# Edge columns of 128 instead of 125 in a graph network kernel

## The chip, the core and the metric
The kernel runs on one core of a Trainium2 chip. TensorE (PE) multiplies matrices, VectorE (DVE) and ScalarE (ACT) compute element by element, GpSimd (POOL) here mostly writes the descriptors of scattering transfers, and SyncE (SP) issues transfers and waits. The metric is the device time of one execution in microseconds (us).

## The reference, cut to what matters
A stack of four graph layers over one graph of 3125 nodes with 256 features and 50000 edges, which are sorted by destination:
```
dst sorted; src, edge_weight permuted with it
# L0: msgs = w[:, None] * h[src]; agg = segment_sum(msgs, dst); z = (1 + eps) * h + agg
#     then twice: linear layer, batch norm over the nodes, relu
x = x + L0(relu(layernorm(x)), src, dst, w)
x = x + L1(relu(layernorm(x)), src, dst, w)   # two weighted graph convolutions, root features, a linear layer
x = x + L2(relu(layernorm(x)), src, dst)      # one unweighted convolution with degree norms
x = x + L3(relu(layernorm(x)), src, dst)      # attention with 4 heads, graph norm, attention with 1 head
```
In every layer a message goes along each edge. The kernel turns the edge list into two dense matrices over pairs of nodes once, the sum of weights W[dst, src] and the count of edges C[dst, src], and all layers multiply by these.

## The kernel before
**The table of pairs.** `pairs` lies in HBM: for each of 25 blocks of 125 destinations, 128 rows of 3200 places, each place two floats (weight, count). SP zeroes it block by block (25 transfers of 3200 KB, lines 484 to 496, four in flight). Behind the table lie 2 x 8 x 128 trash places.

**The edges.** The three lists (dst, src, weight) are loaded as 100 rows of 500 consecutive edges (lines 471 to 473). DVE works out each edge's block and its key, which is the place in the table (lines 1552 to 1568). TensorE turns the rows, so that each list stands as 400 columns of 125 edges. A round is four columns, 500 consecutive edges, so there are 100 rounds.

**The merge.** A scattering transfer may not name one place twice. For each column `same` (line 1586) compares the keys of its edges with those of the columns from it to the end of its round, TensorE adds up weights and counts of equal keys (`sums`, line 870), and `merged` (line 1599) writes value and key: one edge of those with equal keys keeps the sum, the others get a key in the trash places. It works on 8 columns, two rounds, a time (50 times). Columns have 125 edges and the transfers 128 rows, so POOL presets the last three rows of value and key (lines 674 to 677) with zero and trash keys.

**The scatter.** POOL goes through the 100 rounds (line 712 on). In each it issues four indirect transfers (line 744), one column each, that add 128 pairs of floats to their places. Ahead of a round it waits for the merge, for enough zeroed blocks (`zero_ok`), and inside the round for the landing of earlier transfers: ahead of the third transfer the last two of the round before last, ahead of the fourth the first two of the last round. Rounds whose destinations touch wait for more (`rwait`, `rfirst`: flags that DVE works out from the lowest and highest destination of the rounds). After the first of these two waits it raises `rounds_done` by one.

**The consumers.** Layer 0 takes the table in groups of blocks (SIZES 4, 4, 4, 4, 4, 2, 2, 1), each in five parts. For the first part of a group SP waits until `rounds_done` has reached the number of rounds that touch those blocks (`rneed`, line 504), then for its buffer, and loads rows of the table (line 510). TensorE multiplies them with the features (line 931) and turns them (line 951), ACT copies what is turned and stores it as dense matrices. After the last group come the batch norm and all other layers, which read only those dense matrices.

**Order on SP.** The three edge lists, two blocks of zeroing, the features (line 478, 4.5 us on), the other zeroing, then the loads of rows with the weights between them.

Of the kernel before, what the change touches and what calls it, by code (L numbers as in the profile page):

```python
# [5 lines left out]
ALU = mybir.AluOpType  # L6
# [15 lines left out]
EC = E // Q  # L22
# [6 lines left out]
EA = 4  # L29
ECC = EC // EA  # L30
# [90 lines left out]
def gnn_stack(nc, x, src, dst, edge_weight, eps0, W01, b01, g01, be01, W02, b02, g02, be02,  # L121
              W11, b11, W12, b12, Wl1, bl1, root_idx, W2, b2, W31, as31, ad31, b31, gnw, gnb, gnms,
              W32, as32, ad32, b32, out):
    with ExitStack() as ctx:
# [11 lines left out]
        pairs = nc.dram_tensor("pairs", (TRASH + 2 * SC * 128, 2), F32, kind="Internal").ap()  # L136
# [111 lines left out]
        landed = PT[:, 800:800 + NMG]  # L248
        rwait = B[:, S0 + 8 * ECC:S0 + 10 * ECC].rearrange("p (k t) -> p k t", k=2).bitcast(I32)
        rfirst = B[:, S0 + 10 * ECC:S0 + 10 * ECC + 8].bitcast(I32)  # L250
        CW = EA * Q
# [8 lines left out]
        key = Fb[0:Q, 7 * CW:7 * CW + EC]  # L260
        wgt = Fb[0:Q, 7 * CW + EC:7 * CW + 2 * EC]
        keyd = Fb[0:Q, 7 * CW + 2 * EC:7 * CW + 3 * EC]
        vals = Fb[0:Q, 7 * CW + 3 * EC:7 * CW + 5 * EC].bitcast(BF16).rearrange("p (c t) -> p c t", t=4)
# [11 lines left out]
        e1f, e2f = [Hf[0:Q, k * CW:k * CW + EC] for k in (2, 3)]  # L275
        bneed = sb("bneed", [128, NMG], I32)

        M0 = 2 * N
        W = SC * Q
        TRI = R[0:Q, M0:M0 + CW]  # L280
        TW = [R[0:Q, M0 + CW + i * (W // 2):M0 + CW + (i + 1) * (W // 2)].bitcast(BF16) for i in range(SC)]

# [187 lines left out]
        def _(sp):  # L470
            sp.dma_start(dst_i, dst.rearrange("(c k) -> c k", k=CW)).then_inc(S("dst_in"), 16)
            sp.dma_start(src_i, src.rearrange("(c k) -> c k", k=CW)).then_inc(S("src_in"), 16)
            sp.dma_start(wgt_c, edge_weight.rearrange("(c k) -> c k", k=CW)).then_inc(S("wgt_in"), 16)


            def features_in():
                for p0, p1 in PART:
# [8 lines left out]
            sp.dma_start(pairs[TRASH:TRASH + 2 * SC * 128, :].rearrange("(p c) t -> p (c t)", p=128),  # L486
                         R[:, 0:4 * SC]).then_inc(S("zero_tail"), 16)
# [174 lines left out]
        def _(pool):  # L662
# [24 lines left out]
            g.iota(landed[0:1, :], pattern=[[32, NMG // LAND], [0, LAND]], base=0, channel_multiplier=0,  # L687
# [21 lines left out]
            for k in range(NMG):  # L709
                if k == 0:  # L710
                    pool.wait_ge(S("first_merged"), 1)
                elif k == 1 or k % 2 == 0:
                    pool.wait_ge(S("merged"), k // 2 + 1)
                if k < ZREG:
                    blocks = pool.value_load(bneed[0:1, k:k + 1], min_val=1, max_val=NB)
                    pool.wait_ge(S("zero_ok"), blocks)
                    pool.sem_inc(S("begun"), 1)
                elif k == ZREG:
                    pool.wait_ge(S("zero_ok"), NB)
                if k >= 2:  # L720
                    first_two(k - 2)
                if k == 1:
                    pool.wait_ge(S("rwait_made"), 3)
                if 1 <= k <= FIRST_ROUNDS:
                    landed_first = pool.value_load(rfirst[0:1, k - 1:k], min_val=1, max_val=2 * FIRST_ROUNDS + 1)
                    pool.wait_ge(S("early_ok"), landed_first)
                    pool.sem_inc(S("begun"), 1)
                elif k:
                    one = pool.value_load(rwait[0:1, 0, k - 1:k], min_val=32, max_val=32 * (NMG // LAND))
# [4 lines left out]
                    two = pool.value_load(rwait[0:1, 1, k - 2:k - 1], min_val=32, max_val=32 * (NMG // LAND))  # L734
# [72 lines left out]
        def _(pe):  # L807
# [40 lines left out]
            pe.wait_ge(S("wgt_in"), 16)  # L848
            for a in range(EA):
                last = tr(ps[0:Q, 5, a * ECC:(a + 1) * ECC], wgt_c[:, a * Q:(a + 1) * Q], ident[0:ECC, 0:ECC])  # L850
            last.then_inc(S("edge_pe"), 1)
            pe.wait_ge(S("edge_dve"), 1)
            for a in range(EA):
                last = tr(ps[0:Q, 4, a * ECC:(a + 1) * ECC], key_c[:, a * Q:(a + 1) * Q], ident[0:ECC, 0:ECC])
# [7 lines left out]
            def key_rows(t):  # L862
                if t >= 2:
                    pe.wait_ge(S("same_made"), SC * (t - 1))
                for c in range(SC):
                    k = key[:, t * SC + c:t * SC + c + 1]
                    last = tr(ps[0:Q, (t % 2) * 2 + c // 4, c % 4 * Q:(c % 4 + 1) * Q], k.to_broadcast([Q, Q]),
                              ident[0:Q, 0:Q])
                last.then_inc(S("rows_made"), 1)


            def sums(t):
                if t >= 2:
                    pe.wait_ge(S("merged"), t - 1)
                for c0 in range(SC):
                    pe.wait_ge(S("same_made"), SC * t + c0 + 1)
                    for c in range(c0, c0 // MG * MG + MG):
                        last = mm(ps[0:Q, sum_bank(t, c), c * 4:(c + 1) * 4], TW[c0][:, c * Q:(c + 1) * Q],  # L878
                                  vals[:, t * SC + c0, :], start=c0 == c and (c == 0 or t == 0 and c == MG), stop=c0 == c,
                                  skip_group_check=True)  # L880
                    last.then_inc(S("same_used"), 1)
# [438 lines left out]
        def _(act):  # L1320
# [8 lines left out]
            wgt_rows = ps[0:Q, 5, 0:EC].rearrange("p (i c) -> p i c", i=EA)  # L1329
# [212 lines left out]
        def _(dve):  # L1542
# [3 lines left out]

            v_.memset(R[:, 0:2 * ROW // ZR], 0.0).then_inc(S("zero_made"), 1)
# [4 lines left out]
            def block_of(out_, in_i, tmp):  # L1552
# [9 lines left out]
            dve.wait_ge(S("src_in"), 16)  # L1562
# [5 lines left out]
            cp(key.rearrange("p (c i) -> p i c", i=EA), ps[0:Q, 4, 0:EC].rearrange("p (i c) -> p i c", i=EA))\  # L1568
                .then_inc(S("edge_dve"), 1)
            link.mark(v_.tensor_reduce(out=span[0:ECC, 0:1], in_=e1, axis=AX_X, op=ALU.max))  # L1570
            link.mark(v_.tensor_reduce(out=span[0:ECC, 1:2], in_=e1[:, 0:3 * Q], axis=AX_X, op=ALU.max))
            link.mark(v_.tensor_reduce(out=span[0:ECC, 2:3], in_=e1[:, 0:Q], axis=AX_X, op=ALU.min))
            link(v_.tensor_reduce(out=span[0:ECC, 3:4], in_=e1[:, Q:CW], axis=AX_X, op=ALU.min))
# [4 lines left out]
            link.mark(tt(keyd.rearrange("p (t i) -> p t i", i=2 * SC), key.rearrange("p (t i) -> p t i", i=2 * SC),  # L1578
                         both[0:Q, :].unsqueeze(1).to_broadcast([Q, NSC // 2, 2 * SC]), ALU.subtract))
            dve.wait_ge(S("edge_pe"), 3)  # L1580
            ts(bneed[0:1, :], ps[0:1, 7, 0:ECC], 1.0, None, ALU.add).then_inc(S("need_made"), 1)
            dve.wait_ge(S("pool_consts"), 9)
# [17 lines left out]
            def merged(t, c0=0, c1=SC, name="merged"):  # L1600
# [5 lines left out]
                sums = ps[0:Q, sum_bank(t, c0), 4 * c0:4 * c1].rearrange("p (c t) -> p c t", t=4)  # L1606
                n_ = later[0:Q, t % 2, c0:c1]
                kf = keyf[0:Q, t % 2, c0:c1]
                link.mark(v_.tensor_reduce(out=val[0:Q, cc, 0], in_=sums[:, :, 0:3], axis=AX_X, op=ALU.add))
                link.mark(cp(val[0:Q, cc, 1], sums[:, :, 3]))  # L1610
# [678 lines left out]
```

## Time and profile before
| | us |
|---|---|
| median of 3 runs (lowest, highest) | 3661.48 (3661.09, 3667.85) |
| the profiled execution, its own time | 3660.92 |
| its span | 3659.2 |
| PE busy | 3365.4 |
| DVE busy | 2298.8 |
| ACT busy | 849.9 |
| POOL busy | 808.0 |
| line 744, 400 indirect transfers, busy | 618.5 |

The profile is of one execution. Times count from the start of its span. An engine's busy time leaves out waits and the issue of transfers; "idle before" of an instruction is the time in which its engine had nothing, and the name behind it is what ended that. SPq is the queue of SP: a row of it is the issue of a transfer, and its duration is that of the issue, not of the data. The landing of data is told apart.

### The profile page before, as it was taken

The numbers are of one execution on the slowest core, as the hardware profiler recorded it, in microseconds if no ns is written. First come the engines' busy times: TensorE is split into PE (matmuls) and PEld (weight loads), VectorE is DVE, ScalarE is ACT, GpSimd is POOL, SyncE is SP. The second block draws the span as 40 slices with busy tenths as digits, with TensorE's granted clock in tenths as the row PEclk, the third lists the DMA queues.
The fourth block names the chain that finished last, engine by engine and source line by source line (L and its number), as shares of the span: only waits on it lengthen the run. The fifth ranks groups of instructions, "written<-read, shape, count | busy, mean of one in ns | idle before, by whom it ended". The sixth has DMA issues, their size and how long they took to land.

```text
span 3659.2 us, 34305 instructions
## 1 busy us (share of the span) xinstructions
PE 3365.4 (92%) x12633; PEld 1922.0 (53%) x12633; DVE 2298.8 (63%) x3036; ACT 849.9 (23%) x1116; POOL 808.0 (22%) x661
## 2 busy tenths in 40 slices
PE   8999965987999999999839999999999999997998
PEld 7897754764544554545424444444444444464444
DVE  9963321345010111434798888888888899877987
ACT  1113322334000000222112222222222223242222
POOL 5888888840000000000111111111111000010000
PEclk6569987998999999999959999999999999998999
DMA  9999976993444344222456555555555432284422
GB/s 343 364 328 256 303 211 166 302 249 93 137 127 138 119 137 139 90 80 59 127 163 165 119 128 136 121 129 119 136 118 130 111 93 70 68 301 130 124 67 65
DMA packets 279136, 572.59 MB, mean 156 GB/s; under 512 B 93393, under 2 KB 157671, under 8 KB 276921
## 3 DMA queue, kind: packets, MB, share of 16 engines
q1 hardware_dynamic: 140777, 432.89, 37.0%
q0 software_dynamic: 85712, 77.51, 13.2%
q10 hardware_dynamic: 52480, 60.01, 5.6%
q8 instruction: 100, 1.64, 0.2%
q14 instruction: 67, 0.55, 0.0%
HBM read 365.44 MB, written 204.87 MB: 156 GB/s over the span
## 4 chain that ended last, share of the span: by engine, by line
PE 43%; DVE 7%; issue 3%; DMA 1%; ACT 1%; DVEq 0%; ACTq 0%; POOLq 0%
PE ps L1239 29%; PE ps L1078 3%; PE ps L1203 2%; PE ps L1267 2%; PE ps L1246 2%; DVE R L2161 2%; DVE wB L2124 1%; DMA den_d<-R 1%; DVE PT L1956 1%; DVE wA L1956 1%; PE ps L1031 1%; DVE Fb L1956 1%; PE ps L1139 0%; PE ps L1269 0%; DVE PT L2124 0%
## 5 line engine op out<-in xcount | busy, mean ns | idle before, releaser
L1239 PE MATMUL ps<-R,B 125*128 125x500 f32 x2800 | 1092.7, 542 | 32.3 <-DVE R L2161 26.3
L1239 PEld LDWEIGHTS ps<-R,B 125*128 125x128 f32 x2800 | 504.0, 190 | 593.6 <-issue 551.0
L744 POOL DMA_INDIRECT pairs<-w x400 | 618.5, 1546 | 150.0 <-issue 103.6
L1078 PE MATMUL ps<-R,H 125*128 125x500 f32 (+1 forms) x1400 | 543.1, 543 | 15.1 <-ACT H L1350 7.6
L1477 ACT ACTIVATE R<-R,asc 125x1625 f32<-125x1625 f32 (+1 forms) x200 | 320.2, 1601 | 987.2 <-DVE R L2148 987.2
L2148 DVE SCALAR_TENSOR_TENSOR R<-H,asc 125x1625 f32<-125x1625 f32 (+1 forms) x200 | 369.0, 1846 | 141.4 <-PE ps L1246 115.5
L2161 DVE SCALAR_TENSOR_TENSOR R<-R 125x1625 f32<-125x1625 f32 (+1 forms) x250 | 445.0, 1780 | 0.0
L1078 PEld LDWEIGHTS ps<-R,H 125*128 125x128 f32 x1400 | 253.6, 191 | 283.7 <-issue 280.8
L931 PE MATMUL ps<-R,H 125*128 125x375 f32 (+1 forms) x1000 | 303.7, 451 | 76.5 <-DMA R<-pairs 76.0
L774 POOL DMA_DIRECT2D den_d<-R x138 | 117.4, 851 | 794.2 <-DVE R L2161 746.7
L1239 PE MATMUL ps<-R,H 125*128 125x500 f32 (+1 forms) x700 | 274.2, 548 | 19.3 <-DVE R L2161 17.5
L1715 DVE TENSOR_TENSOR Fb<-Fb,ps 128x250 f32<-128x250 f32 (+1 forms) x140 | 67.2, 480 | 335.8 <-PE ps L931 269.5
L1078 PE MATMUL ps<-R,B 125*128 125x500 f32 (+1 forms) x700 | 266.8, 538 | 1.6 <-ACT R L1434 0.9
L931 PEld LDWEIGHTS ps<-R,H 125*128 125x128 f32 x1000 | 186.9, 195 | 153.0 <-DMA R<-pairs 76.6
L1956 DVE SCALAR_TENSOR_TENSOR Fb<-R,asc,Fb 125x1625 f32<-125x1625 uint16 (+1 forms) x144 | 265.2, 1841 | 0.0
L757 POOL DMA_DIRECT2D Fb<-ct_d x9 | 4.9, 546 | 982.6 <-PE ps L1031 759.6
L1239 PEld LDWEIGHTS ps<-R,H 125*128 125x128 f32 x700 | 126.2, 192 | 160.6 <-issue 131.0
L1078 PEld LDWEIGHTS ps<-R,B 125*128 125x128 f32 x700 | 127.1, 190 | 140.4 <-issue 139.2
L951 PE MATMUL ps<-ident,R 125*125 125x125 f32 x1250 | 169.8, 284 | 23.2 <-ACT B L1390 17.0
L1596 DVE SCALAR_TENSOR_TENSOR R<-ps,Fb,R 125x500 bf16<-125x500 f32 (+3 forms) x400 | 190.9, 536 | 0.0
L951 PEld LDWEIGHTS ps<-ident,R 125*125 125x125 f32 x1250 | 160.3, 195 | 43.8 <-ACT B L1390 22.0
L878 PE MATMUL ps<-Fb,R 125*125 125x4 bf16 x1000 | 128.0, 247 | 20.7 <-DVE R L1596 19.1
(317 smaller groups left out, 3045.1 us busy)
## 6 DMA issues: line engine op xcount, KB each, us to landing
pairs<-R SPq DMA_DIRECT2D x25, 3200.0 KB, 28.3
R<-ct_d SPq DMA_DIRECT2D x162, 406.2 KB, 3.5
R<-pairs SPq DMA_DIRECT2D x25, 2500.0 KB
R<-ct_d SPq DMA_DIRECT2D x162, 375.0 KB, 3.1
R<-wt_d SPq DMA_DIRECT2D x50, 812.5 KB, 4.3
R<-wt_d SPq DMA_DIRECT2D x50, 750.0 KB, 4.2
den_d<-R POOLq DMA_DIRECT2D x75, 312.5 KB, 5.5
den_d<-R POOLq DMA_DIRECT2D x75, 250.0 KB, 4.7
```

The lines of the kernel that those rows point to most:

```text
L744: pool.indirect_dma_start(pairs, bass.IndirectOffsetOnAxis(ap=key_u[:, c:c + 1], axis=0), val[:, c, :], None, compute_op=ALU.add)\
L774: pool.dma_start(den_d[a][k % 2], TT[q % TR][:, 8 * Q:w], accum_op=ALU.add).then_inc(S(f"den_sum{a}"), 16)
L878: last = mm(ps[0:Q, sum_bank(t, c), c * 4:(c + 1) * 4], TW[c0][:, c * Q:(c + 1) * Q], vals[:, t * SC + c0, :], start=c0 == c and (c == 0 o ...
L931: last = mm(ps[:, n % 4, 0:w], H[0:Q, j0 + m, k * 128:(k + 1) * 128], pair_rows_at(i)[0:Q, m, o:o + w, 0], start=m == 0, stop=m == nb - 1 ...
L951: last = tr(ps[0:Q, 4 + 2 * (n % 2) + t, m * Q:(m + 1) * Q], pair_rows_at(i)[0:Q, m, b * Q:(b + 1) * Q, t], ident[0:Q, 0:Q])
L1078: last = mm(ps[:, bank, at:at + w], rows[0:Q, j, f * 128:(f + 1) * 128], TL[q % TS][0:Q, o:o + w], start=j == 0 and at == 0, stop=j == NB ...
L1239: last = mm(ps[:, bank, at:at + w], rows[0:Q, j, f * 128:(f + 1) * 128], TT[q % TR][0:Q, o:o + w], start=j == 0 and at == 0, stop=j == NB ...
L1477: a(t, t, ACT.Exp, bias=s2).then_inc(S("l3_exp"), 1)
L1596: stt(TW[c][:, b * CW + lo:(b + 1) * CW], ps[0:Q, (t % 2) * 2 + b, lo:CW], k, TRI[:, 0:CW - lo], ALU.is_equal, ALU.mult, accum_out=later[0 ...
L1956: stt(dst, t, score, dst, ALU.min, ALU.max).then_inc(S(name), 1)
L2148: stt(TT[q % TR][0:Q, 0:w], u[0:Q, 0:w], s8, u[0:Q, w:2 * w], ALU.add, ALU.max).then_inc(S("l3_a"), 1)
L2161: stt(t, t, 1.0, lc, ALU.min, ALU.mult).then_inc(S("l3_t"), 1)
```

## The change
The edges stand in columns of 128 (EP), in rows of 512 (CW). That makes 98 rows, 392 columns and 98 rounds (49 merges of two rounds). The last row has 336 edges and 176 padded places.

- The lists are loaded as 96 rows in one transfer each, and the last two rows (512 and 336 edges) by one transfer each: nine transfers where there were three. Ahead of the six SP waits for three memsets of DVE that fill the padded places: destination 3125, source 2048, weight 0. This key is the place TRASH + 2048, behind the trash places, for which `pairs` grows by 128 places.
- POOL no longer presets rows 125 to 127 of values and keys.
- All tiles of the merge have 128 partitions and columns of 128; comparisons are up to 512 wide instead of 500. They start at 5000 instead of 6250 in R. The subtraction of trash keys has an instruction of its own for the 49th merge.
- The constants of `landed` keep 100 entries; the rest follows from ECC = 98.

```diff
-EC = E // Q
+EP = 128
+EA = 4
+CW = EA * EP
+ECC = -(-E // CW)
+EC = EA * ECC
+EFULL = ECC // 32 * 32
+ELAST = E - (ECC - 1) * CW
+EPAD = 2048
...
-            sp.dma_start(dst_i, dst.rearrange("(c k) -> c k", k=CW)).then_inc(S("dst_in"), 16)
-            sp.dma_start(src_i, src.rearrange("(c k) -> c k", k=CW)).then_inc(S("src_in"), 16)
-            sp.dma_start(wgt_c, edge_weight.rearrange("(c k) -> c k", k=CW)).then_inc(S("wgt_in"), 16)
+            edge_lists = ((dst_i, dst, "dst_in"), (src_i, src, "src_in"), (wgt_c, edge_weight, "wgt_in"))
+            for t, e, name in edge_lists:
+                sp.dma_start(t[0:EFULL, :], e[0:EFULL * CW].rearrange("(c k) -> c k", k=CW)).then_inc(S(name), 16)
+            sp.wait_ge(S("edge_pad"), 3)
+            for t, e, name in edge_lists:
+                for c in range(EFULL, ECC):
+                    w = CW if c < ECC - 1 else ELAST
+                    sp.dma_start(t[c:c + 1, 0:w], e[c * CW:c * CW + w].rearrange("(c k) -> c k", c=1)).then_inc(S(name), 16)
...
-            g.memset(val, 0.0).then_inc(S("pool_consts"), 1)
-            pool.wait_ge(S("trash_made"), 1)
-            g.tensor_copy(key_u.rearrange("p (t i) -> p t i", i=2 * SC), both.unsqueeze(1).to_broadcast([128, NSC // 2, 2 * SC]))\
-                .then_inc(S("pool_consts"), 1)
...
-            pe.wait_ge(S("wgt_in"), 16)
+            pe.wait_ge(S("wgt_in"), 16 * (1 + ECC - EFULL))
...
+            v_.memset(dst_i[EFULL:ECC, ELAST:CW], N).then_inc(S("edge_pad"), 1)
+            v_.memset(src_i[EFULL:ECC, ELAST:CW], EPAD).then_inc(S("edge_pad"), 1)
+            v_.memset(wgt_c[EFULL:ECC, ELAST:CW], 0.0).then_inc(S("edge_pad"), 1)
             v_.memset(R[:, 0:2 * ROW // ZR], 0.0).then_inc(S("zero_made"), 1)
...
-            dve.wait_ge(S("dst_in"), 16)
+            dve.wait_ge(S("dst_in"), 16 * (1 + ECC - EFULL))
...
-                lo, b = c % MG * Q, c // MG
-                stt(TW[c][:, b * CW + lo:(b + 1) * CW], ps[0:Q, (t % 2) * 2 + b, lo:CW], k, TRI[:, 0:CW - lo],
-                    ALU.is_equal, ALU.mult, accum_out=later[0:Q, t % 2, c:c + 1]).then_inc(S("same_made"), 1)
+                lo, b = c % MG * EP, c // MG
+                stt(TW[c][:, b * CW + lo:(b + 1) * CW], ps[0:EP, (t % 2) * 2 + b, lo:CW], k, TRI[:, 0:CW - lo],
+                    ALU.is_equal, ALU.mult, accum_out=later[0:EP, t % 2, c:c + 1]).then_inc(S("same_made"), 1)
```

## Rows read from the trace of the kernel before

**Rows 1.** Stretches: us; busy PE, PEld, DVE, ACT, POOL; PEclk; DMA share; GB/s
```profile
598.00:643.00 45.00, 2.27 (x18) 2.01 (x17) 0.42 (x1) 2.02 (x4) 37.68 (x25) 0.55 0.41 68
...
832.00:3659.00 2827.00, 2663.10 (x8723) 1333.09 (x8721) 1888.92 (x1705) 640.96 (x659) 179.56 (x239) 0.97 0.44 121
```

**Rows 2.** Waits of PE, 0:850 and 505:600 us: total, times, longest
```profile
PE ps L931 <- DMA R<-pairs: 76.0, 3, 43.2
...
PE ps L931 <- DMA R<-pairs: 28.5, 1, 28.5
```

**Rows 3.** Timeline of PE, 590 to 860 us: start, duration, what [idle before]
```profile
598.25 2.01 PE L951 MATMUL ps<-ident,R 125*125 125x125 f32 x16
...
643.43 7.15 PE L931 MATMUL ps<-R,H 125*128 125x375 f32 x16 [43.16 <-DMA R<-pairs]
...
764.61 5.29 PE L931 MATMUL ps<-R,H 125*128 125x375 f32 x8 [4.39 <-DMA R<-pairs]
...
803.72 1.09 PE L951 MATMUL ps<-ident,R 125*125 125x125 f32 x8
```

**Rows 4.** Timeline of SP, its issues of the loads of scattered rows
```profile
516.18 0.91 SPq L510 DMA_DIRECT2D R<-pairs  x2
...
634.40 25.35 SPq L510 DMA_DIRECT2D R<-pairs  x3
...
756.24 18.77 SPq L510 DMA_DIRECT2D R<-pairs  x5
...
789.15 20.06 SPq L510 DMA_DIRECT2D R<-pairs  x5
```

**Rows 5.** Waits of SP's queue, 630:660, 745:780 and 780:850 us
```profile
SPq L504 <- POOLq L740: 61.8, 1, 61.8
...
SPq L504 <- POOLq L740: 29.5, 1, 29.5
...
SPq L504 <- POOLq L750: 13.3, 1, 13.3
```

**Rows 6.** Line 744: its group in 0:850; source view of 400:790
```profile
L744 POOL DMA_INDIRECT pairs<-w x400 | 618.5, 1546 | 150.0 <-issue 103.6 <-SPq L493 25.4 <-DMA pairs<-w 20.8
...
L744 POOL DMA_INDIRECT pairs<-w x206: 1543/1545/1563, 400.1 to 780.9; - x103
...
DMA to landing us min/median/max: 2.9/6.8/9.7
```

**Rows 7.** Timeline of POOL, the first transfer and two of the middle
```profile
38.68 1.82 POOL L744 DMA_INDIRECT pairs<-w  x1 [24.75 <-SPq L493]
...
400.05 1.55 POOL L744 DMA_INDIRECT pairs<-w  x1 [0.30 <-issue]
...
401.90 1.54 POOL L744 DMA_INDIRECT pairs<-w  x1 [0.30 <-issue]
```

**Rows 8.** Timeline of SP at the start
```profile
0.82 0.41 SPq L471 DMA_DIRECT2D Fb<-in_dst  x1
...
1.62 0.34 SPq L473 DMA_DIRECT2D Fb<-in_edge_weight  x1
...
4.53 22.05 SPq L478 DMA_DIRECT2D X<-in_x  x2
...
26.63 1.13 SPq L479 DMA_DIRECT2D idx_i<-in_L_gnn_root_idx  x1
```

**Rows 9.** Timeline of DVE at the start
```profile
1.56 0.07 DVE L1548 MEMSET later<- 128x16 f32 x1
...
3.80 1.65 DVE L1554 CAST Fb<-Fb 100x500 f32<-100x500 int32 x1 [2.02 <-DMA Fb<-in_dst]
...
17.86 0.16 DVE L1613 TENSOR_TENSOR w<-keyf,trash 125x4 uint32<-125x4 f32 x1
```

**Rows 10.** Line 1596, 500 wide, in 0:850; timeline of PE
```profile
L1596 DVE SCALAR_TENSOR_TENSOR R<-ps,Fb,R 125x500 bf16<-125x500 f32 x100 | 72.8, 728 | 0.0
...
246.13 3.60 PE L817 MATMUL ps<-ident,H 125*128 125x125 f32 x16 [0.75 <-DVE w L1613]
```

More of the change, by code:

```diff
@@ L133, in sb @@
             return ctx.enter_context(nc.sbuf_tensor(name, shape, dt))
-        pairs = nc.dram_tensor("pairs", (TRASH + 2 * SC * 128, 2), F32, kind="Internal").ap()
+        pairs = nc.dram_tensor("pairs", (TRASH + (2 * SC + 1) * 128, 2), F32, kind="Internal").ap()
         wt_d = nc.dram_tensor("wt_d", (NB, 128, N), F32, kind="Internal").ap()
@@ L247, in gnn_stack @@
         touch = B[:, S0 + 4 * ECC:S0 + 8 * ECC].rearrange("p (k t) -> p k t", k=4)
-        landed = PT[:, 800:800 + NMG]
+        landed = PT[:, 800:900]
         rwait = B[:, S0 + 8 * ECC:S0 + 10 * ECC].rearrange("p (k t) -> p k t", k=2).bitcast(I32)
         rfirst = B[:, S0 + 10 * ECC:S0 + 10 * ECC + 8].bitcast(I32)
-        CW = EA * Q
         src_i = Fb[0:ECC, 0:CW].bitcast(I32)
@@ L259, in gnn_stack @@
         esrc = Hf[0:ECC, 0:CW]
[L260 to L263, printed above, removed]
+        key = Fb[0:EP, 7 * CW:7 * CW + EC]
+        wgt = Fb[0:EP, 7 * CW + EC:7 * CW + 2 * EC]
+        keyd = Fb[0:EP, 7 * CW + 2 * EC:7 * CW + 3 * EC]
+        vals = Fb[0:EP, 7 * CW + 3 * EC:7 * CW + 5 * EC].bitcast(BF16).rearrange("p (c t) -> p c t", t=4)
         key_u = w31[:, 0, 0:EC].bitcast(U32)
@@ L274, in gnn_stack @@
         keyf = sb("keyf", [128, 2, SC])
-        e1f, e2f = [Hf[0:Q, k * CW:k * CW + EC] for k in (2, 3)]
+        e1f, e2f = [Hf[0:EP, k * CW:k * CW + EC] for k in (2, 3)]
         bneed = sb("bneed", [128, NMG], I32)
[L278 to L281, printed above, removed]
+        M0 = 5000
+        W = SC * EP
+        TRI = R[0:EP, M0:M0 + CW]
+        TW = [R[0:EP, M0 + CW + i * (W // 2):M0 + CW + (i + 1) * (W // 2)].bitcast(BF16) for i in range(SC)]
         att1 = [B[:, 0:WIDE], B[:, WIDE:2 * WIDE]]
@@ L485, in _ @@
             zero = R[:, 0:2 * ROW // ZR].unsqueeze(1).to_broadcast([128, ZR, 2 * ROW // ZR])
-            sp.dma_start(pairs[TRASH:TRASH + 2 * SC * 128, :].rearrange("(p c) t -> p (c t)", p=128),
-                         R[:, 0:4 * SC]).then_inc(S("zero_tail"), 16)
+            sp.dma_start(pairs[TRASH:TRASH + (2 * SC + 1) * 128, :].rearrange("(p c) t -> p (c t)", p=128),
+                         R[:, 0:2 * (2 * SC + 1)]).then_inc(S("zero_tail"), 16)
             for i in range(NB + ZQ):
@@ L686, in _ @@
                    allow_small_or_imprecise_dtypes=True).then_inc(S("pool_consts"), 1)
-            g.iota(landed[0:1, :], pattern=[[32, NMG // LAND], [0, LAND]], base=0, channel_multiplier=0,
+            g.iota(landed[0:1, :], pattern=[[32, 100 // LAND], [0, LAND]], base=0, channel_multiplier=0,
                    allow_small_or_imprecise_dtypes=True).then_inc(S("pool_consts"), 1)
@@ L728, in _ @@
                 elif k:
-                    one = pool.value_load(rwait[0:1, 0, k - 1:k], min_val=32, max_val=32 * (NMG // LAND))
+                    one = pool.value_load(rwait[0:1, 0, k - 1:k], min_val=32, max_val=32 * (100 // LAND))
                     pool.wait_ge(S(f"first_two{(k - 1) % LAND}"), one)
@@ L733, in _ @@
                     pool.sem_inc(S("begun"), 1)
-                    two = pool.value_load(rwait[0:1, 1, k - 2:k - 1], min_val=32, max_val=32 * (NMG // LAND))
+                    two = pool.value_load(rwait[0:1, 1, k - 2:k - 1], min_val=32, max_val=32 * (100 // LAND))
                     pool.wait_ge(S(f"last_two{(k - 2) % LAND}"), two)
@@ L847, in _ @@
             tr = nc.tensor.transpose
[L848 removed]
+            pe.wait_ge(S("wgt_in"), 16 * (1 + ECC - EFULL))
             for a in range(EA):
[L850 removed]
+                last = tr(ps[0:EP, 5, a * ECC:(a + 1) * ECC], wgt_c[:, a * EP:(a + 1) * EP], ident[0:ECC, 0:ECC])
             last.then_inc(S("edge_pe"), 1)
@@ L853, in _ @@
             for a in range(EA):
-                last = tr(ps[0:Q, 4, a * ECC:(a + 1) * ECC], key_c[:, a * Q:(a + 1) * Q], ident[0:ECC, 0:ECC])
+                last = tr(ps[0:EP, 4, a * ECC:(a + 1) * ECC], key_c[:, a * EP:(a + 1) * EP], ident[0:ECC, 0:ECC])
             last.then_inc(S("edge_pe"), 1)
@@ L866, in key_rows @@
                     k = key[:, t * SC + c:t * SC + c + 1]
-                    last = tr(ps[0:Q, (t % 2) * 2 + c // 4, c % 4 * Q:(c % 4 + 1) * Q], k.to_broadcast([Q, Q]),
-                              ident[0:Q, 0:Q])
+                    last = tr(ps[0:EP, (t % 2) * 2 + c // 4, c % 4 * EP:(c % 4 + 1) * EP], k.to_broadcast([EP, EP]),
+                              ident[:, :])
                 last.then_inc(S("rows_made"), 1)
@@ L877, in sums @@
                     for c in range(c0, c0 // MG * MG + MG):
-                        last = mm(ps[0:Q, sum_bank(t, c), c * 4:(c + 1) * 4], TW[c0][:, c * Q:(c + 1) * Q],
+                        last = mm(ps[0:EP, sum_bank(t, c), c * 4:(c + 1) * 4], TW[c0][:, c * EP:(c + 1) * EP],
                                   vals[:, t * SC + c0, :], start=c0 == c and (c == 0 or t == 0 and c == MG), stop=c0 == c,
@@ L1567, in _ @@
             dve.wait_ge(S("edge_pe"), 2)
-            cp(key.rearrange("p (c i) -> p i c", i=EA), ps[0:Q, 4, 0:EC].rearrange("p (i c) -> p i c", i=EA))\
+            cp(key.rearrange("p (c i) -> p i c", i=EA), ps[0:EP, 4, 0:EC].rearrange("p (i c) -> p i c", i=EA))\
                 .then_inc(S("edge_dve"), 1)
             link.mark(v_.tensor_reduce(out=span[0:ECC, 0:1], in_=e1, axis=AX_X, op=ALU.max))
-            link.mark(v_.tensor_reduce(out=span[0:ECC, 1:2], in_=e1[:, 0:3 * Q], axis=AX_X, op=ALU.max))
-            link.mark(v_.tensor_reduce(out=span[0:ECC, 2:3], in_=e1[:, 0:Q], axis=AX_X, op=ALU.min))
-            link(v_.tensor_reduce(out=span[0:ECC, 3:4], in_=e1[:, Q:CW], axis=AX_X, op=ALU.min))
+            link.mark(v_.tensor_reduce(out=span[0:ECC, 1:2], in_=e1[:, 0:3 * EP], axis=AX_X, op=ALU.max))
+            link.mark(v_.tensor_reduce(out=span[0:ECC, 2:3], in_=e1[:, 0:EP], axis=AX_X, op=ALU.min))
+            link(v_.tensor_reduce(out=span[0:ECC, 3:4], in_=e1[:, EP:CW], axis=AX_X, op=ALU.min))
             dve.sem_inc(S("edge_dve"), 1)
@@ L1577, in _ @@
             both = trash[:, :, :].rearrange("p a i -> p (a i)")
-            link.mark(tt(keyd.rearrange("p (t i) -> p t i", i=2 * SC), key.rearrange("p (t i) -> p t i", i=2 * SC),
-                         both[0:Q, :].unsqueeze(1).to_broadcast([Q, NSC // 2, 2 * SC]), ALU.subtract))
+            EV = NSC // 2 * 2 * SC
+            link.mark(tt(keyd[:, 0:EV].rearrange("p (t i) -> p t i", i=2 * SC), key[:, 0:EV].rearrange("p (t i) -> p t i", i=2 * SC),
+                         both.unsqueeze(1).to_broadcast([EP, NSC // 2, 2 * SC]), ALU.subtract))
+            link.mark(tt(keyd[:, EV:EC], key[:, EV:EC], trash[:, 0, :], ALU.subtract))
             dve.wait_ge(S("edge_pe"), 3)
             ts(bneed[0:1, :], ps[0:1, 7, 0:ECC], 1.0, None, ALU.add).then_inc(S("need_made"), 1)
-            dve.wait_ge(S("pool_consts"), 9)
+            dve.wait_ge(S("pool_consts"), 7)
             link.mark(cp(bminf[0:1, :], ps[0:1, 7, ECC:2 * ECC]))
@@ L1605, in merged @@
                 cc = slice(t * SC + c0, t * SC + c1)
[L1606 to L1610, printed above, removed]
+                sums = ps[0:EP, sum_bank(t, c0), 4 * c0:4 * c1].rearrange("p (c t) -> p c t", t=4)
+                n_ = later[0:EP, t % 2, c0:c1]
+                kf = keyf[0:EP, t % 2, c0:c1]
+                link.mark(v_.tensor_reduce(out=val[0:EP, cc, 0], in_=sums[:, :, 0:3], axis=AX_X, op=ALU.add))
+                link.mark(cp(val[0:EP, cc, 1], sums[:, :, 3]))
                 link.join()
                 link(stt(kf, n_, 1.0, keyd[:, cc], ALU.is_equal, ALU.mult))
-                tt(key_u[0:Q, cc], kf, trash[0:Q, t % 2, c0:c1], ALU.add).then_inc(S(name), 1)
+                tt(key_u[0:EP, cc], kf, trash[0:EP, t % 2, c0:c1], ALU.add).then_inc(S(name), 1)
             def stats_of(j):
```

6 lines of the change are left out of this document (2 added, 4 removed).

## The prediction
> **What bounds the kernel now.** I read the table by stretches first. In 598 to 643 us TensorE is busy 2.27 of 45 us while POOL is busy 37.68; from 832 us on TensorE is busy 2663 of 2827 us and POOL has nothing to do with it [rows 1]. So the change touches only the first 832 us, and its worth is how much earlier that part ends. The waits of TensorE in it tell of three stops for a load of the scattered rows (`R<-pairs`), together 76.0 us: 28.5 us near 525, 43.2 us at 643 and 4.4 us at 764 [rows 2, 3]. The timeline of TensorE gives their places: nothing between 600.3 and 643.43, then nearly unbroken work to 760.2, the 4.39 us stop, and then no such stop when the last group begins, right behind the work that ends at 804.8 [rows 3].
>
> The loads before those stops are issued at 516.18, 634.40, 756.24 and 789.15 [rows 4]. SP waited 61.8 us for POOL's round counter ahead of the one at 634.40, 29.5 us ahead of the one at 756.24, 13.3 us ahead of the last [rows 5]. These are the gates "this many rounds have landed". Counting the destinations that the seed draws, the groups of SIZES need 16, 32, 48, 64, 80, 88, 96 and 100 rounds of 500 edges. The trace agrees: 634.40 - 516.18 = 118.22 us for 16 rounds is 7.39 us a round, and POOL issues a transfer each 1.85 us (400.05, 401.90), so 7.40 a round [rows 4, 7]. Gate 88 then opens at 693.6 and gate 96 at 752.8 (634.40 + 8 and 16 x 7.40); the load at 756.24 came 3.4 us after its gate, held by its buffer, which TensorE frees. The load for gate 100 (789.15) lands some 8 us later, at 797, while TensorE is busy until 804.8: 7.6 us of slack.
>
> So the last binding gate is the one of 80 rounds, at 634.40, and everything later hangs on TensorE's work from 643.43 on. What counts is when round 80's count is reached, and whether the gates behind it move as far.
>
> **Part 1, fewer rounds.** With 512 edges a round, the same destination list gives needs of 16, 31, 47, 63, 78, 86, 94 and 98 (39,842 edges lie below block 20; over 512 that is 77.8, over 500 it was 79.7). The gate of 80 becomes 78, 88 becomes 86, 96 becomes 94, 100 becomes 98: two rounds each, so the stretch behind 634.40 moves as one piece. Two rounds are 8 transfers of 1.85 us (1545 ns and a gap of 0.30 us [rows 6, 7]): 14.8 us. The gate before it (64 becomes 63) moves by one round, 7.4 us; it only starts work that ends 43 us before it is needed.
>
> Cost of one transfer after: it describes 128 rows before and after (three of the 128 aimed at trash rows), and in the second half of the stage all 206 took 1543 to 1563 ns [rows 6]. Bounds: nothing, or in proportion to real rows, 128/125, +37 ns x 312 transfers up to gate 78 = 11.5 us. A gain has no source, since no row shows a transfer that is shorter for fewer rows. I take 0, since the time does not move at all over transfers with different keys.
>
> **Part 2, the rows of the edge lists.** Three loads of 100 rows become three of 96 and six of one row, all ahead of the zeroing on SP's queue. SP's third load took 0.34 us, and the zeroing's first issues follow back to back; the dearest small issue in that stretch is 1.13 us (idx_i) [rows 8]. Six issues at 0.38 us (0.34 and a gap of 0.04) are 2.3 us; bounds 2.0 (6 x 0.34) and 7.0 (6 x 1.17). I take 2.3, from the row of the same kind of load in the same empty queue. It matters because POOL's first transfer, at 38.68, ended a wait of 24.75 us for SP [rows 7], and SP got there late because its issues of the feature load (22.05 us for two) ran at the pace of the DMA engines [rows 8]. A start of the zeroing later by 2.3 us is thus first scatter later by 2.3 us, all rounds behind it too. Bounds of this step: 0, if the edge rows were taking engine time from the zeroing that is now given back, and the 7.0 above. The wait on edge_pad that is put ahead of the six costs nothing: DVE's small memset at 1.56 took 0.07 us [rows 9], three more from 1.02 are over by 1.6, ahead of SP's arrival at 2.0. They push zero_made by as little, ahead of SP's need of it at 4.3; what is queued behind the wait on SP are the six loads and the zeroing, nothing else.
>
> The Trainium skill ("DMA: Bandwidth & Descriptors", Anatomy of one DMA) gives a fixed cost of about 2.0 us for every DMA, which speaks against splitting a load into pieces. The trace's pieces overlap: issues stand 0.3 to 0.5 us apart while their data lands later. Were the page's cost paid one after the other, six pieces would cost an estimated 12 us and the time would be near 3659.
>
> **Part 3, the edge lists arrive later.** DVE and TensorE wait for all three loads of a list, so the key chain starts some 1.5 to 3 us later than its 3.80 [rows 9]. The first merge was ready at 18.0 (17.86 + 0.16), 20.7 us before the first transfer started [rows 7, 9]. Cover is ample; without it the cost would be those 3 us.
>
> **Part 4, wider columns.** A merge column's comparison goes from 500 to 512 elements. The 500-wide one takes 728 ns [rows 10]; by width 512/500 it would be 745, and there are 392 instead of 400. +2.4% on each of 98% as many is nothing: the DVE stage ends, and TensorE's first products start, about where they do (246.13 [rows 10]). Bounds: -2% and +2.4% of 230 us, -5 and +5.5. Neither is seen: the gate at 516 leaves TensorE 28.5 us of idle time, the next 43.2 [rows 2], which also hold the 2.3 us by which zeroing ends later. POOL needs a merge of 8 columns each 14.8 us; 50 of them between 18.0 and 246.1 are one each 4.6.
>
> **Part 5, what POOL drops.** Its memset of val and the copy into key_u go; both stood ahead of the 24.75 us wait for SP, so that they gave cover and gain nothing [rows 7]. The padded places all carry one key beyond the scattered rows and value 0, and 176 of them sit in the last round; TensorE's merge leaves one of them per key, as it does for any key. The wait flags between rounds stay off: by the destination list no last node of three columns reaches into the next round in either layout.
>
> **Sum.** -14.8 + 2.3 = -12.5 us. Profiled span 3659.2 - 12.5 = 3646.7; the run's own time was 3660.92, 1.72 above its span, so 3648.4; the median of the runs shown is 0.56 above that run, so **3649**.
>
> **Rivals.**
> (1) *The start costs more.* SP stops at each small load at the dearest rate of rows 8: 7.0 us, net -7.8, time 3653.7. For it: idx_i's 1.13 us. Against: that one was issued into a full queue. Further out, if each row load ran alone from issue to landing (dst_in: issued 0.82, used at 3.80, 3.0 us [rows 8, 9]), 17.9 us, net +3.1, time 3664.6. Against: three such loads were issued between 0.82 and 1.96.
> (2) *The tail behind gate 78 doesn't move as one piece.* The stop at 764 (4.39 us) comes from a buffer, and 28 us of work behind 804 share the DMA engines with ACT's stores, which can fall otherwise. At most 4.4 us either way: 3645 to 3653.5. The case that gate 80 falls by one round only (79) would be 3656.3; 77.8 against 78 is 94 edges of margin, so I don't expect it.
> (3) *Slower: the transfers begin to wait for their landing.* Before the third transfer of a round POOL waits for the last two of the round before last, before the fourth for the first two of the last round. The nearer of these is 6 transfers, 11.1 us, behind the issue it waits for; landing takes 6.8 us in the median and 9.7 at most [rows 6]. Three more real rows in each would have to lift the usual landing above 11.1 us; every further 0.13 us a round then eats 12.5 us over 98 rounds. At 11.6 us the cost is 49 us and the time 3698. For it: 33 transfers of the second half already ended their gap on such a landing. Against: that gap was still the usual 0.30 us, and 2.4% more rows make 9.7 into 9.9.
> (4) *It does nothing that counts*, because TensorE is the bound between the gates: against it stands 43.2 us of idle time; time 3661 to 3664.
>
> **Chances.** Forecast (3645 to 3652) 0.68; rival 1, 0.12; rival 2 beyond that, 0.10; rival 3, 0.05; rival 4 and what I have not seen, 0.05. A measurement of this kernel can tell 0.2%, 7.3 us, from no change. Below 3654.2 lie the forecast, most of rivals 1 and 2: faster 0.81. Same 0.13. Slower 0.06. The range of 8 in 10 takes the forecast with both ends of the start's cost (0 gives 3646.7, 7.0 gives 3653.7), 4.4 us of the tail below and above: 3643 to 3658.
>
> **What would show it.** Right: 392 transfers at 1545 ns, first near 41, last near 768.5; the load behind the fourth gate at 622 with TensorE idle some 36 us before 631; the stop of 4.4 us still there; the last group's work ending at 819; from there the same 2827 us. Wrong: a first transfer well after 43 (rival 1), gaps above 0.30 us ended by a landing (rival 3), a load gate at 629 (79 rounds), or a tail that starts 12 us early and ends less early (rival 2).

## The result, and the profile after

The changed kernel takes 3648.85 us in the median (3648.03 to 3655.97, 6 runs), the kernel before 3661.84 beside it: ratio 0.9963, 95% interval 0.9953 to 0.9974. That is 0.37% or 13 us faster; forecast were 3649 and 12.5 us. The profiled span is 3646.9 us; 3646.7 was worked out.

The scatter of the changed kernel, by the view of its line (now 749):
```profile
L749 POOL DMA_INDIRECT pairs<-w x392: 1537/1545/1815, 41.9 to 768.7; - x196
...
  SPq L502: 28.5, 2
  DMA pairs<-w: 13.7, 35
```
There are 392 transfers at the same 1545 ns [rows 6]. The first starts at 41.9 us and the last at 768.7; before it was 38.68 [rows 7] and 780.95. So the start is 3.2 us later, the end 12.25 us earlier, and in between 8 transfers of 1.85 us are gone (14.8) and the idle time of POOL beyond the usual gaps is 0.65 us less.

The start, in the timeline of the changed kernel (start, duration, what):
```profile
2.20 0.60 SPq L482 DMA_DIRECT2D Fb<-in_dst  x2
...
3.42 0.55 SPq L482 DMA_DIRECT2D Fb<-in_edge_weight  x2
...
4.42 1.52 SPq L504 DMA_DIRECT2D pairs<-R  x2
...
5.98 20.94 SPq L487 DMA_DIRECT2D X<-in_x  x2
...
26.96 2.78 SPq L488 DMA_DIRECT2D idx_i<-in_L_gnn_root_idx  x1
```
The six row loads take SP from 2.20 to 3.97; the zeroing starts at 4.42 instead of 2.42. In the issue of the features most of these 2.0 us vanish (it ends at 26.92 instead of 26.58 [rows 8]), the load of `idx_i` takes 2.78 us instead of 1.13, and when SP comes back to the zeroing, at 30.74 instead of 28.75, it is 2.0 us late again. The 1.2 us that are missing to 3.2 are lost after that, in the issues of the third and the fourth block of zeroing: 10.2 us, where they took 9.0. The fourth, in the kernel before and in the changed one:
```profile
30.50 7.20 SPq L495 DMA_DIRECT2D pairs<-R  x1
```
```profile
31.41 9.49 SPq L504 DMA_DIRECT2D pairs<-R  x1
```
Only when it is through, at 37.70 and at 40.90, does SP report the first zeroed block, for which POOL waits; POOL's first transfer starts 1.0 us later in both kernels.

The gates in the changed kernel, first SP's issues behind those of 78, 94 and 98 rounds, then the timeline of PE:
```profile
623.14 0.91 SPq L519 DMA_DIRECT2D R<-pairs  x2
...
743.88 0.36 SPq L519 DMA_DIRECT2D R<-pairs  x1
...
779.09 0.81 SPq L519 DMA_DIRECT2D R<-pairs  x2
```
```profile
593.56 2.01 PE L956 MATMUL ps<-ident,R 125*125 125x125 f32 x16
632.58 8.28 PE L936 MATMUL ps<-R,H 125*128 125x375 f32 x16 [37.00 <-DMA R<-pairs]
...
749.96 2.91 PE L936 MATMUL ps<-R,H 125*128 125x375 f32 x8 [0.65 <-DMA R<-pairs]
...
793.60 1.49 PE L936 MATMUL ps<-R,H 125*128 125x375 f32 x4
...
823.78 24.09 PE L835 MATMUL ps<-R,wA 128*128 128x500 f32 x56 [4.75 <-ACT R L1409]
```
Against [rows 3, 4]: the load behind the 78 round gate leaves 11.3 us earlier (634.40 to 623.14), TensorE begins with it 10.9 us earlier, and its stop there is 37.0 us where it was 43.2. The next stop is 0.65 us where it was 4.39; the last group begins 11.05 us earlier. The first product of the following stage (line 835, before 830 at 837.03) begins 13.25 us earlier. From there on the changed kernel takes 2823.1 us, the kernel before 2822.2.

### The profile page after: what moved, and what is told of

It reads as the page before. It is cut to its first block, busy times and chain, and to the rows that moved or that the text cites. A ratio compares the mean times of both kernels' runs of the same rounds, so it can differ in the third digit from the quotient of the medians.

```text
span 3646.9 us, 34205 instructions
## 1 busy us (share of the span) xinstructions
PE 3304.7 (91%) x12605; PEld 1842.6 (51%) x12605; DVE 2296.6 (63%) x3020; ACT 850.0 (23%) x1116; POOL 794.2 (22%) x651
## 4 chain that ended last, share of the span: by engine, by line
PE 42%; DVE 7%; issue 4%; DMA 1%; ACT 1%; POOL 0%; DVEq 0%; ACTq 0%; POOLq 0%
PE ps L1244 29%; PE ps L1083 3%; PE ps L1208 2%; PE ps L1272 2%; PE ps L1251 2%; DVE R L2171 2%; DVE wB L2134 1%; DVE PT L1966 1%; DVE wA L1966 1%; PE ps L1036 1%; DVE Fb L1966 0%; DMA den_d<-R 0%; PE ps L1274 0%; DVE PT L2134 0%; PE ps L1184 0%
## 5 line engine op out<-in xcount | busy, mean ns | idle before, releaser
L749 POOL DMA_INDIRECT pairs<-w x392 | 606.2, 1546 | 150.4 <-issue 107.9
L1606 DVE SCALAR_TENSOR_TENSOR R<-ps,Fb,R 128x512 bf16<-128x512 f32 (+3 forms) x392 | 190.2, 544 | 0.0
L883 PE MATMUL ps<-Fb,R 128*128 128x4 bf16 x980 | 73.4, 173 | 79.1 <-DVE R L1606 69.5
```

Of the source, the lines that this page charges most:

```text
L883: last = mm(ps[0:EP, sum_bank(t, c), c * 4:(c + 1) * 4], TW[c0][:, c * EP:(c + 1) * EP], vals[:, t * SC + c0, :], start=c0 == c and (c == ...
L1606: stt(TW[c][:, b * CW + lo:(b + 1) * CW], ps[0:EP, (t % 2) * 2 + b, lo:CW], k, TRI[:, 0:CW - lo], ALU.is_equal, ALU.mult, accum_out=later[ ...
```

## The experiments

Beside them the kernel before takes 3665 to 3668 us, so each is told by its ratio to the runs of before beside it. One thousandth is 3.7 us, and the intervals are about as wide as that to either side; where two kernels lie closer, I go by the places of the stops in the traces.

**The change once more.**

> The changed kernel as it is, timed once more beside the others, so that the experiments have it on their chip. Against the kernel before 0.9955 to 0.9972.

3653.78 us, ratio 0.9963 (0.9955 to 0.9972): the first result again. Its profile has the first transfer at 41.8 and the 78 round stop ending at 632.33, so these two places repeat within 0.3 us from run to run. What lies behind them does not: the next stop is 1.65 us long instead of 0.65, and line 835 begins at 825.90 instead of 823.78.
```profile
751.38 2.91 PE L936 MATMUL ps<-R,H 125*128 125x375 f32 x8 [1.65 <-DMA R<-pairs]
```
This is the measure for all others.

**Who pays for the six row loads.**
```diff
 # SP: the six loads of single rows are gone; ACT, first thing:
+            act.wait_ge(S("edge_pad"), 3)
+            for t, e, name in ((dst_i, dst, "dst_in"), (src_i, src, "src_in"), (wgt_c, edge_weight, "wgt_in")):
+                for c in range(EFULL, ECC):
+                    act.dma_start(t[c:c + 1, 0:w], ...)
```


> The changed kernel, with the six loads of single rows issued by ACT instead of SP. The theory is that the six loads cost time only because SP issues them ahead of the zeroing: the zeroing's first issue then falls from 4.42 back to about 2.9 us (it now waits for DVE's memset, which ends at 2.3), POOL's first transfer from 41.9 to between 39 and 40.5, and the time from 3648.9 to 3646 to 3647.5. The rival, that the later first transfer comes from the DMA queue behind the features and not from SP's issue of the rows, expects the first transfer at 41.9 and the time unchanged.

3649.41 us, ratio 0.9950 (0.9936 to 0.9963), 4.8 us below the change. Timeline of SP and PE:
```profile
2.72 1.58 SPq L499 DMA_DIRECT2D pairs<-R  x2
...
628.40 7.78 PE L931 MATMUL ps<-R,H 125*128 125x375 f32 x16 [37.45 <-DMA R<-pairs]
```
The zeroing's first issue is at 2.72, the first transfer at 39.8, 2.0 us earlier than in the change, and the gate's stop ends at 628.4, 3.9 to 4.2 us earlier (the scatter also had fewer stops on landings). So what SP issues ahead of the zeroing is what delays the scatter. Against the kernel before, the zeroing starts 0.3 us later here and the first transfer 1.1 us later, so 0.8 of the 1.2 us that I had not foreseen are still lost, wherever the rows are issued. Why is open.

**The other side: twelve row loads.**
```diff
-  sp.dma_start(t[c:c + 1, 0:w], ...)
+  for o, v in ((0, w // 2), (w // 2, w - w // 2)):
+      sp.dma_start(t[c:c + 1, o:o + v], ...)
```


> The changed kernel with each of the six single rows loaded in two halves, so twelve small loads on SP ahead of the zeroing instead of six. The theory (the small loads cost what SP spends on issuing them, six took 1.8 us) expects the zeroing's first issue at 6.2 instead of 4.4, POOL's first transfer at 43.7 to 44.5, and the time 1.8 to 2.6 us above the changed kernel's. The rival that the start's 3.2 us came from the queue behind the features expects less than 0.5 us. A cost of 2 us for each small load would be 12 us.

Zeroing from 6.20, as expected; first transfer at 43.3, 1.5 us later (a little under the 1.8 of the theory); the gate's stop ends at 635.44, 3.1 us later. The time is 3654.39 us, ratio 0.9965 (0.9953 to 0.9978), 0.7 us above the change: too little for the interval to show. A small load costs SP's 0.3 us of issue (1.8 us for six), far from 2 us each.

**Four more transfers, ahead of the gate and behind it, to adjacent places.** These two kernels and the next two also make their further operands at the start; their first transfer stays at 41.8 to 42.1.
```diff
+                if k in (40,):            # (95,) in the second kernel
+                    for m in range(4):
+                        pool.indirect_dma_start(pairs, <128 adjacent places of their own>, <zeros>, compute_op=ALU.add)
```


> The changed kernel with four more indirect transfers of 128 rows behind round 40, all of zeros, to places of their own behind the table. The theory (each transfer ahead of the 78 round gate costs POOL's 1.85 us and nothing else) expects the gate's load and everything later 7.4 us later: 3656.2. The rival that the transfers are not the bound between the gates expects no change, 3648.9; one by which a further transfer also lengthens the landing waits expects clearly more than 3657.

> The same four transfers, but behind round 95, so after the gates of 78, 86 and 94 rounds and ahead of that of 98. The theory (the last binding gate is that of 78, and the last load has some 7 us of slack) expects at most 1 us: its load leaves at 786.5 instead of 779.1, lands near 794.5, and TensorE is ready for it at 793.6; time 3649 to 3650. The rival, that the end of the scatter sets the time, expects 7.4 us: 3656.2.

Ahead of the gate: 3667.19 us, ratio 1.0000 (0.9991 to 1.0009), 13.5 us above the change, twice what I expected. Behind it: 3658.55 us, ratio 0.9978 (0.9968 to 0.9988), 5.5 us, also more. The second kernel's timeline of POOL, and then the view of the line of its four transfers, say why:
```profile
774.29 1.54 POOL L758 DMA_INDIRECT pairs<-w  x1 [0.30 <-issue]
780.27 1.54 POOL L758 DMA_INDIRECT pairs<-w  x1 [4.43 <-DMA pairs<-w]
```
```profile
DMA to landing us min/median/max: 10.2/13.3/15.0
```
POOL issues the four at 1.85 us each as any other, but they land after 10.2 to 15.0 us, where real ones take 6.8 in the median [rows 6]. Real transfers behind them then wait for landings: here the last one for 4.43 us. In the first kernel the landings of the four are not shown; POOL's idle time beyond the usual gaps is 5.7 us more there than in the change, which is nearly the surplus of 6.1. The experiment had changed two things, the count and the spread of the places; so neither number is the price of a plain transfer.

**The same with spread places.**
```diff
+                if k == 40:               # k == 97 in the second kernel
+                    for m in range(4):
+                        c = (k - 3) * MG + m
+                        pool.indirect_dma_start(pairs, <keys of column c>, <zeros>, compute_op=ALU.add)
```


> Four more transfers ahead of round 40 as in the second experiment, still of zeros, but to the places of round 37's keys, so spread as real ones are. There the transfers to 128 adjacent places cost 13.0 us instead of 7.4, and landed after 10.2 to 15.0 us where real ones take 7.5. The theory that the surplus came from the slow landing on adjacent places and the price of a plain transfer is 1.85 us expects 7.4 us here: the 78 round gate's stop ends at 640.0 instead of 632.6, and the time is 7 to 9 us above the changed kernel's. The rival that any four further transfers clog the queue expects 12 to 13 us again.

> The four zero transfers, spread over the places of round 94's keys, ahead of round 97, so behind the gates of 78, 86 and 94 rounds. In the third experiment four transfers to adjacent places behind round 95 held the last real transfer by 4.1 us and moved the last load by 12.3 us, which cost 5.6 us where the last group begins. The theory (the last load has about 7 us of slack, so 7.4 us more in the queue are nearly hidden) expects the last load's issue near 786.5 instead of 779.1, at most 1 to 2 us where the last group begins, and a time 0 to 2 us above the changed kernel's, ratio to before 0.9963 to 0.9969. The rival, that the end of the scatter sets the time, expects 7.4 us, ratio 0.9984, as ahead of the gate (0.9986).

Ahead of the gate: 3661.28 us, ratio 0.9986 (0.9977 to 0.9995), 8.4 us above the change; 7.4 were expected. Behind the gate: 3651.60 us, ratio 0.9966 (0.9952 to 0.9979), 1.1 us above it. Timelines of PE, first the kernel with four ahead, then the one with four behind:
```profile
641.41 7.49 PE L945 MATMUL ps<-R,H 125*128 125x375 f32 x16 [35.45 <-DMA R<-pairs]
...
764.83 4.59 PE L945 MATMUL ps<-R,H 125*128 125x375 f32 x8 [7.28 <-DMA R<-pairs]
```
```profile
631.86 8.43 PE L945 MATMUL ps<-R,H 125*128 125x375 f32 x16 [36.39 <-DMA R<-pairs]
...
795.93 1.59 PE L945 MATMUL ps<-R,H 125*128 125x375 f32 x4 [2.37 <-DMA R<-pairs]
```
Four transfers ahead move the gate's stop from 632.3 or 632.6 to 641.4. Four behind leave it where it was, and the last group, which had no stop, gets one of 2.37 us (its load left at 788.85, where I had expected 786.5). So four transfers ahead of the 78 round gate cost 8.4 us, near the 7.4 of their issue (the interval of the ratio is 3.3 us to either side), and four behind the gate of 94 rounds are nearly free.

A transfer between the gates of 78 and of 94 rounds was not tried. The traces speak against its being free. In the changed kernel TensorE has finished at 749.31 what it has, and the load behind the 94 round gate is there at 749.96, so there is no slack. And in the kernel with four ahead the second line shows what a later count does: there SP got the count of 94 rounds at 755.3 instead of 743.7 and TensorE stood for 7.28 us, where the changed kernel stands for 0.65 and its repetition for 1.65. In that one execution the following stage begins 11.9 us later than in the repetition, more than the 8.4 us of all its runs.

**Where the scatter starts.** In the change POOL waits 28.2 us for SP ahead of its first transfer.
```diff
-ZAHEAD = 2
+ZAHEAD = 6
```


> The changed kernel with the features loaded behind the first six blocks of zeroing instead of behind two. The theory that POOL's first transfer stands 28 us behind its operands only because SP is stuck in the issue of the features expects the first transfer at 18 to 22 us instead of 41.9, and, since TensorE idles 37 us ahead of the 78 round gate, nearly all of that in the time: 3626 to 3631, if neither the second zeroed block nor the merges, which wait for the features at the seventh merge, hold POOL up later. The rival is that they do: the second block is then reported only behind the features, near 46, and the merges stop until the features land, so that POOL loses 5 to 20 us again and the time is 3632 to 3648.

3637.64 us, ratio 0.9918 (0.9905 to 0.9932), 16.5 us below the change. First transfer at 23.48 (expected 18 to 22), gate's stop down to 13.0 us and over at 614.36. DVE waited 31.4 us for the features, but POOL had merges enough. What held POOL to 23.5 was SP again: it reports the first zeroed block only when the issue of the fourth is through, here at 22.50.

```diff
-ZAHEAD = 2
-ZQ = 4
+ZAHEAD = 6
+ZQ = 2            # and the rows on ACT
```


> The changed kernel with three edits: rows on ACT, the features behind six blocks of zeroing, and two blocks of zeroing in flight instead of four. In the fourth experiment the first transfer stood at 23.5, held by SP, which has to get the fourth block into its queue before it reports the first. With two in flight the first block (landed near 13.5) is reported before the third is issued, and the first merge (17.4) becomes the last to come. Theory: first transfer at 18 to 19, the 78 round gate's stop down to about 8 us, time 4 to 6 us below the fourth experiment's, that is 17 to 20 us below the changed kernel. The rival: with two in flight the zeroing runs slower or the merges, which wait for the features, hold POOL up, and the gain is under 2 us.

3634.26 us, ratio 0.9917 (0.9904 to 0.9929): no gain on the last. The first transfer came only to 20.77 (expected 18 to 19), and those 2.7 us were given back in stops on landings: the gate's stop ends at 614.70. The first block was reported at 13.3 as planned, but the first merge came at 18.27 and the first transfer another 2.5 us behind it. Its rival had foreseen so small a gain, but neither of its reasons is what the trace shows. With four in flight and the rows on ACT:

> The changed kernel with the single rows on ACT and the features behind six blocks of zeroing, four blocks in flight. Rows on ACT alone took 2.0 us off the first transfer and 4.8 us off the time against the changed kernel, features late alone 18.4 us off the first transfer and 16.5 us off the time. If the gains add up, the first transfer is at 21.5 and the ratio to before 0.9905 to 0.9913. If the landing stops in the scatter eat the earlier start, as they did when the first transfer came at 20.8 (ratio 0.9917), it stays at 0.9917.

3631.68 us, ratio 0.9914 (0.9900 to 0.9927), the lowest ratio of all, 18 us below the change. First transfer at 21.88, the gate's stop ends at 614.23:
```profile
478.19 1.54 POOL L744 DMA_INDIRECT pairs<-w  x1 [2.27 <-DMA pairs<-w]
...
614.23 8.41 PE L931 MATMUL ps<-R,H 125*128 125x375 f32 x16 [16.62 <-DMA R<-pairs]
```
The gate's stop ends where the two others have it, so the gains of the two edits do not add up there: an extra 2.27 us stop on a landing at 478 took most of the 1.6 us by which the start was ahead. By time the three kernels cannot be told apart. What makes single transfers land so late is open.

**The width of the weights.**
```diff
-                        last = mm(ps[0:EP, ...], TW[c0][:, c * EP:(c + 1) * EP],
+                        last = mm(ps[0:Q, ...], TW[c0][:, c * EP:c * EP + Q],
```


> The changed kernel with the merge's weight matrices cut to 125 of their 128 columns, so that the sums of three edges in each column are left out. In the changed kernel the load of such a matrix takes 111 ns where it took 219, and TensorE is busy 100 of 150 us in 50 to 200 us where it was busy 137. The theory that the width of 128 does this expects 215 to 225 ns and 135 to 140 us again, whichever clock is granted there. The rival, that it is the granted clock (1.0 in the changed kernel's stretch, 0.5 in that before), expects 111 ns where the clock is 1.0. Either way the span stays within 3 us, since the scatter is far behind the merges.

Groups of the merge's weight loads in 50 to 200 us (busy, mean ns of one), in the kernel before, the change, this kernel and the one with rows on ACT:
```profile
L878 PEld LDWEIGHTS ps<-Fb,R 125*125 125x125 bf16 x641 | 82.3, 222 | 16.2 <-DVE R L1596 15.4 <-issue 0.6
```
```profile
L883 PEld LDWEIGHTS ps<-Fb,R 128*128 128x128 bf16 x640 | 37.1, 111 | 65.6 <-DVE R L1606 51.4 <-issue 5.6
```
```profile
L883 PEld LDWEIGHTS ps<-Fb,R 128*125 128x125 bf16 x640 | 82.5, 220 | 20.3 <-DVE R L1607 18.9 <-issue 1.1
```
```profile
L878 PEld LDWEIGHTS ps<-Fb,R 128*128 128x128 bf16 x640 | 37.0, 110 | 65.9 <-DVE R L1606 49.4 <-issue 7.8
```
With 125 columns 220 ns, at a granted clock of 1.0 (2.4 GHz) in that stretch; with 128 columns 110 ns, at a granted clock of 0.5 (1.2 GHz) in the kernel with rows on ACT. So the width does it, and the clock does not show in it. The span was 3647.4 us, as expected: this stage is not on the path. The loads of FP32 matrices in the same stretch, in the kernel before and in this one, whose FP32 matrices kept 128 columns:
```profile
L867 PEld LDWEIGHTS ps<-ident,Fb 125*125 125x125 f32 x264 | 59.5, 333 | 0.0
```
```profile
L872 PEld LDWEIGHTS ps<-ident,Fb 128*128 128x128 f32 x258 | 53.9, 237 | 0.0
```
They too take about 100 ns less with 128 columns than with 125 (226 ns in the changed kernel).

## Why the prediction was right

**The gate of 80 rounds.** It is right that this gate makes the long stop, and that transfers ahead of it have a price: four cost 8.4 us. Wrong is "the last binding gate is the one of 80 rounds". The prediction takes the load at 756.24 for one "held by its buffer", and the stop at 764 for one that "comes from a buffer". But SP had waited 29.5 us for POOL's counter ahead of that load [rows 5]. The views of the line that ends this wait give its time, in the kernel before (line 504, 745 to 780 us) and in the changed one (line 513, 735 to 750 us):
```profile
L504 SPq EVENT_SEMAPHORE  x1: 17/17/17, 756.1 to 756.1; - x1
```
```profile
L513 SPq EVENT_SEMAPHORE  x1: 17/17/17, 743.7 to 743.7; - x1
```
The loads left 0.15 us later, at 756.24 and 743.88, without a wait for a buffer. So this was the gate of 96 (now 94) rounds, which opened 3.4 us later than 16 rounds of 7.40 us; two stops of POOL on landings, near 736 and 738, are 1.6 us of that. All thirteen profiles have a stop of TensorE behind this gate, from 0.32 to 7.28 us. That the sum came out all the same is because this gate, too, moves by two rounds; the reading was wrong, and it would have misled about a change that touches only the rounds between the two gates.

**Part 1, 14.8 us.** Right: 392 transfers at the same 1545 ns, 8 fewer ahead of both gates that bind. Three more real rows in each cost nothing that shows, the bound of 11.5 us was not needed.

**Part 2, 2.3 us.** The issues themselves were sized well (2.0 us at the zeroing's first issue), but the first transfer came 3.2 us later. The step that failed is "A start of the zeroing later by 2.3 us is thus first scatter later by 2.3 us": SP lost another 1.2 us in the issues of the third and the fourth block of zeroing, behind the features. Most of that loss is there with the rows on ACT too; what makes it is open. The fixed cost of about 2.0 us that the prediction takes from the Trainium skill ("DMA: Bandwidth & Descriptors", Anatomy of one DMA) stands there for transfers issued from GpSimd, and the row loads are issued from SP. Paid one after the other it would have been 12 us for six; six took SP 1.8 us, and six more moved the first transfer by 1.5.

**Part 3, lists later.** Right in that it costs nothing, wrong in the sign. The first merge was due some 1.5 to 3 us later; it was ready at 17.43 instead of 18.02 [rows 9]. DVE starts with the destinations later, but its first operations are shorter (timeline of DVE, the changed kernel first, then the one before):
```profile
4.56 0.70 DVE L1562 CAST Fb<-Fb 98x512 f32<-98x512 int32 x1 [2.10 <-DMA Fb<-in_dst]
5.29 0.43 DVE L1563 TENSOR_SCALAR Fb<-Fb 98x512 f32<-98x512 f32 x1
```
```profile
5.48 0.69 DVE L1555 TENSOR_SCALAR Fb<-Fb 100x500 f32<-100x500 f32 x1
```
The cast takes 0.70 us where it took 1.65 [rows 9], the operation behind it 0.43 where it took 0.69. POOL's memset of val and copy into key_u are gone, so its work of the start is over at 4.97 us instead of 6.62, and in the kernel before the same kind of operation took 0.69 us at 6.21 and 0.42 at 6.93. That POOL's work slowed DVE is argued from this; no run tried it alone.

**Part 4, wider columns.** Right for DVE: 742 ns for the widest comparison, 745 worked out. I had not priced TensorE, whose weight loads became twice as fast. The Trainium skill ("TensorE: Matmul & The Clock Gate", Weight-path perf modes) states that fast weight load is on for 128 weights of a type other than FP32; for bf16 the trace agrees, 111 ns against 220 with 125. It does not fit the FP32 loads, which fell from 333 to 226 ns by going from 125 to 128 columns.

**The tail (rival 2).** It did not move as one piece. The places of [rows 3] moved by 10.9, 14.7 and 11.05 us and the next stage by 13.25. Waits of PE in 749 to 794 us of the change:
```profile
PE ps L956 <- ACT B L1395: 5.0, 4, 4.0
...
PE ps L936 <- DMA R<-pairs: 0.7, 1, 0.7
```
The stop of 4.39 us on a load shrank to 0.65, but one of 4.0 us on ACT stands in its place; in the last group TensorE then came through 2.2 us faster. In sum: 14.8 less the 3.2 of the start are 11.6; 0.75 were lost up to TensorE's start behind the gate, 2.4 won in the tail, 0.95 lost behind it, which leaves 12.3. So 12.3 against 12.5 is closer than the steps are: errors of 1 to 2 us cancelled, which is luck. Each of these places is also read from one execution. From the end of the long stop to line 835 the kernel before takes 193.6 us, the changed one 191.2, and its repetition 193.6 again, so the 2.4 us won in the tail are what differs between two executions and no effect of the change that is shown.

**Rival 3, landing waits.** Nothing like its 49 us happened, but "that gap was still the usual 0.30 us" does not hold for all: the kernel before has stops of 1.58 and 0.62 us on landings near 736 and 738. Beyond 0.30 us each, such stops come to 3.7 us in the kernel before (20.8 us in 57) and 3.2 in the changed one (13.7 in 35). And the runs showed that the mechanism is near: behind four transfers that landed after 10 to 15 us POOL stood for 4.43 us, and four such transfers ahead of the gate cost 13.5 us instead of 8.4.

## What to carry to other kernels

When a chain of equal transfers runs at the pace of their issue, find the last point at which its consumer really waits; the transfers ahead of that point have a price, which is mostly the issue interval, and those behind it are nearly free. Ask of every stop, also of a short one, what released the load behind it: here the last such point was not the gate with the stop of 43 us but the one with 4.39. A transfer's payload is not what it costs there, so fill it. Then look at what holds the chain's first link: here 28 us of the queue stood in front of it, and starting 18 us earlier was worth 16.5 us, more than the fuller columns.

## What the runs showed of the hardware

- Four scattering adds of zeros to 128 adjacent places of 8 bytes each landed after 10.2 to 15.0 us, 13.3 in the median; four to spread places, near the same point of the scatter, after 8.0 to 10.3 us, 8.9 in the median. The real ones take 6.8 us in the median of the second half.
- A weight load of 128 columns in bf16 takes 110 ns, of 125 columns 220 ns, at a granted clock of 0.5 as at 1.0. In FP32 it takes 226 to 237 ns with 128 columns and 333 ns with 125.
- The granted clock in 50 to 200 us was 0.5 (1.2 GHz) in some profiles and 1.0 (2.4 GHz) in others, of kernels with the same work there (rows on ACT 0.5, the change 1.0). What decides it is open; it did not show in the busy time of TensorE there (99.8 and 100.0 of 150 us).
